# GpSimd norms the last head of rows 8 to 15 ahead of its own scaling, and two blocks of values are copied out of PSUM at other rows of VectorE's loop

## Chip, cores, metric

One core of one Trainium2 chip runs the whole program. The metric is the device time of one execution in microseconds. Five engines work side by side, each through its own list of instructions in order: TensorE (PE in the profile, its weight loads PEld), VectorE (DVE), ScalarE (ACT), GpSimd (POOL) and SyncE (SP, which issues transfers). They wait for each other through semaphores.

## What is computed

The reference is a chain of four residual blocks over x of shape 16 x 128 x 256: a gated attention with four heads, a quantized feed-forward, a second attention with 16 heads, and a mixture of experts. The change is where the first block ends. There, every head of 64 numbers is normed and scaled before it is added to x:

```
mean = jnp.mean(h, axis=-1, keepdims=True)
var = jnp.mean((h - mean) ** 2, axis=-1, keepdims=True)
h_norm = (h - mean) * jax.lax.rsqrt(var + 1e-05)
h_norm = h_norm * outnorm_scale.reshape(1, NH, 1, DH)
...
x = x + _L0_xattn_ref(_layernorm(x, axis=-1), ctx_1024, ctx_1024, ...)
x = x + _L0_ffn_ref(_layernorm(x, axis=-1), ...)
```

The quantized feed-forward needs one largest absolute value over the whole normed x before its first product. Beside all this, keys and values of the second attention, which depend on the context alone, are projected early.

## The kernel before

The 16 rows of x ("row" below is one of the NB = 16 blocks of 128 positions x 256 numbers, held with the positions on the 128 partitions) pass through each stage in order. Between 72 and 116 us of the span the engines do this:

- ScalarE norms the heads of row b in place, `head_norm(b)` (L615): four instructions of 128x64 for rows 0 to 7, three for rows 8 to 15 (HB = 8). Between rows it evicts the keys of a chunk of four rows, `keys(c)` (L621): chunk 0 behind row 3, chunk 1 behind row 7, chunk 2 behind row 13, chunk 3 behind all rows.
- GpSimd multiplies row b by the scale, `h_scale(b)` (L468, one 128x256 instruction), when ScalarE has signalled `h_normed` for the row, and for rows 8 to 15 when VectorE has signalled `last_normed` too.
- VectorE walks a loop over t = 0 to 16: `last_head(t + 2)` (L1129, the fourth head of rows 8 to 15), `add_heads(t)` (L1133, x plus the scaled heads, waits for `h_scaled`), `stats2(t - 1)` (L1137, the statistics of the new x). Where t is 6 and 14 it also runs `values_kept(1)` and `values_kept(2)` (L1119): two instructions each, which take the values of a chunk out of the two banks of pC and add a bias.
- TensorE projects keys and values in four chunks, `keys_values(c)`: 8 matmuls of keys (L1674) and 16 of values (L1683). The values of chunk c go into the banks of pC when VectorE has emptied them of chunk c - 1: `pe.wait_ge(s["v_kept"], 2 * (c - 1) + i + 1)`.

Then comes the turn stage. VectorE forms mean and rstd of all rows, norms each into XL (L956) and takes its largest absolute value (L1163), with `values_kept(3)` in between. TensorE transposes each normed row (L1696) and beside it nine pairs of weight blocks (L1608). ScalarE evicts these (L645, L628), behind `keys(3)`, which waits for the last values (`v_done`). At the end TensorE turns the largest values (L1706) once all rows are evicted and VectorE has the maximum of each partition (L1172), and after a few small steps the products of the feed-forward (L1727) begin.

The order within every engine is written out by hand, as the code below shows.

Of the kernel before, what the change touches and what calls it, by code (L numbers as in the profile page):

```python
# [12 lines left out]
ALU = mybir.AluOpType  # L13
# [52 lines left out]
def at(t, b):  # L66

    if isinstance(b, int):
        return t[:, b]
    ap = t[:, bass.ds(b, 1)]  # L70
    return ap.squeeze(1)


def cols(b, n):

    return bass.ds(b * n, n)
# [9 lines left out]
def build(nc, A, out):  # L86
    x_d = A["x"].rearrange("b s d -> s b d")
    ctx_d = A["ctx_1024"].rearrange("b s d -> s b d")
    NB, S, D = A["x"].shape
    KD = D // P  # L90
    NH0 = A["L0_xattn_igate_bias"].shape[0]
    DH0 = D // NH0
# [16 lines left out]
    with ctx:  # L109
        def sb(name, shape, dt=F32):  # L110
            return ctx.enter_context(nc.sbuf_tensor(name, shape, dt))
# [53 lines left out]
        def view(o, *shape):  # L165
            n = int(np.prod(shape))
            names = "abcd"[:len(shape)]
            ap = arena[:, o:o + n]
            if len(shape) == 1:
                return ap  # L170
            kw = {names[k]: shape[k] for k in range(1, len(shape))}
            return ap.rearrange(f"p ({' '.join(names)}) -> p {' '.join(names)}", **kw)
# [4 lines left out]
        HU = view(0, NB, NH0, DH0 + 1)  # L177
# [50 lines left out]
        mean = sb("mean", [P, NB * NH0])  # L228
        rstd = sb("rstd", [P, NB * NH0])
# [59 lines left out]
        s = Sems()  # L289
# [19 lines left out]
        HB = NB // 2  # L309
# [115 lines left out]
        def _(pool):  # L425
# [35 lines left out]

            pool.wait_ge(s["late_in"], 16 * 6)

            def h_scale(b, u, h):
                pool.wait_ge(s["h_normed"], b + 1)
                if b >= HB:
                    pool.wait_ge(s["last_normed"], b - HB + 1)
                nc.gpsimd.tensor_tensor(at(HN, b), at(HN, b), oscale[:, :].rearrange("p (h d) -> p h d", h=NH0), ALU.mult).then_inc(s["h_scaled"], 1)  # L468
            for b in range(NB):
                h_scale(b, 0, 0)  # L470
# [434 lines left out]
        def _(dve):  # L905
            link = chain(dve, "dve_chain")
            V_ = nc.vector
# [208 lines left out]
            def values_kept(c):  # L1116
                for i in range(2):
                    dve.wait_ge(s["v_done"], 2 * c + i + 1)
                    V_.tensor_tensor(V[:, 4 * c + 2 * i:4 * c + 2 * i + 2, :, 0:DH1], pC[:, i, :].rearrange("p (b h d) -> p b h d", b=2, h=NH1),  # L1119
                                     bv[:, :].rearrange("p (h d) -> p h d", h=NH1).unsqueeze(1).broadcast_to([P, 2, NH1, DH1]), ALU.add).then_inc(s["v_kept"], 1)  # L1120
# [4 lines left out]
            values_kept(0)  # L1125
            head_scale(1)

            def last_head(b, u, h):
                V_.tensor_scalar(at(HU, b)[:, NH0 - 1, 0:DH0], at(HU, b)[:, NH0 - 1, 0:DH0], mean[:, cols(b * NH0 + NH0 - 1, 1)], rstd[:, cols(b * NH0 + NH0 - 1, 1)], ALU.subtract, ALU.mult).then_inc(s["last_normed"], 1)  # L1129

            def add_heads(b, u, h):
                dve.wait_ge(s["h_scaled"], b + 1)
                V_.tensor_tensor(at(X, b).rearrange("p (h d) -> p h d", h=NH0), at(X, b).rearrange("p (h d) -> p h d", h=NH0), at(HN, b), ALU.add).then_inc(s["x1_ready"], 1)  # L1133

            def stats2(b, u, h):
                dve.wait_ge(s["x1_ready"], b + 1)
                V_.bn_stats(at(ST, b), at(X, b)).then_inc(s["row_stats"], 1)  # L1137
            for t in range(NB + 1):
                if HB <= t + 2 < NB:
                    last_head(t + 2, 0, 0)  # L1140
                if t < NB:
                    add_heads(t, 0, 0)
                if t >= 1:
                    stats2(t - 1, 0, 0)
                if t in (6, 14):
                    values_kept(1 + t // 14)
            dve.wait_ge(s["row_stats"], NB)
            moments(4, NB, D)

# [252 lines left out]
            u = (NB - 1) % 2  # L1402
# [749 lines left out]
```

## Time and profile before

| what | value |
|---|---|
| median of 3 runs | 599.08 us (598.14 to 599.44) |
| the profiled execution, its own time | 596.75 us |
| its span, first to last instruction | 595.0 us |
| PE busy | 514.5 us, 86% |
| DVE busy | 379.0 us, 64% |
| ACT busy | 324.4 us, 55% |
| POOL busy | 141.0 us, 24% |
| mean granted clock of TensorE | 0.949 |

The shares are means over the span and say little of one stage. In the rows further down, times are in microseconds from the start of the span. In a row of the timeline, the first number is the start and the second the duration, xN says how many like instructions were merged, and the bracket tells how long the engine sat idle before and who released it. The time of an instruction on VectorE includes what it spends blocked after its issue.

### The profile page before, as it was taken

What the parts mean: (1) busy time and instruction counts of PE and PEld (TensorE: products, weight loads), DVE (VectorE), ACT (ScalarE), POOL (GpSimd) and SP (SyncE); (2) the same over time, 40 slices, a digit from 0 to 9 for tenths busy, and PEclk for the clock granted to TensorE, in tenths of its full rate; (3) what the DMA queues carried; (4) which work ended last, traced back from release to release, by engine and by line L of the source; (5) the groups of instructions that cost most, each with busy time, mean ns of one, the idle gap of its engine ahead of it and who ended that gap; (6) DMA issues with size and microseconds to landing.
All of it is one profiled execution on the core that took longest, in us unless ns stands there. A gap on an engine that the chain in (4) does not pass through costs nothing.

```text
span 595.0 us, 9287 instructions
## 1 busy us (share of the span) xinstructions
PE 514.5 (86%) x3284; PEld 362.9 (61%) x3284; DVE 379.0 (64%) x956; ACT 324.4 (55%) x682; POOL 141.0 (24%) x202
## 2 busy tenths in 40 slices
PE   1989997899999502999989999995799999999994
PEld 1568755644444202887657787874667776777673
DVE  6586998854499989779679699987413332143101
ACT  2866496733499969761398899984212112211220
POOL 2025633000000000000323223111235344534431
PEclk9999998999999955799999999998799999999997
DMA  7900000000000000034000101015134535453410
GB/s 227 298 19 1 2 1 1 1 0 1 0 0 1 0 0 1 0 122 162 2 1 1 38 2 37 1 38 177 28 115 120 183 126 199 120 181 123 132 44 22
DMA packets 31994, 37.58 MB, mean 63 GB/s; under 512 B 8656, under 2 KB 27728, under 8 KB 31952
## 3 DMA queue, kind: packets, MB, share of 16 engines
q1 hardware_dynamic: 28880, 29.07, 15.1%
q0 software_dynamic: 3072, 7.95, 4.6%
q8 instruction: 26, 0.43, 0.3%
q14 instruction: 16, 0.13, 0.1%
HBM read 30.14 MB, written 6.88 MB: 62 GB/s over the span
## 4 chain that ended last, share of the span: by engine, by line
PE 67%; DVE 15%; ACT 10%; issue 3%; POOL 2%; DMA 1%; POOLq 0%; DVEq 0%
PE pA L2103 12%; PE pB L2121 9%; PE pC L1772 6%; PE pC L1811 5%; PE pA L1805 3%; PE pB L1821 3%; PE pA L1727 2%; PE pC L1727 2%; PE pB L1727 2%; ACT XIT L712 2%; PE pC L2114 2%; DVE am L1220 2%; PE pB L1901 2%; DVE arena L1216 2%; DVE am L1186 2%
## 5 line engine op out<-in xcount | busy, mean ns | idle before, releaser
L480 POOL TENSOR_TENSOR arena<-KT,par 128x256 f32<-128x256 f32 x32 | 19.0, 613 | 248.7 <-DVE XIT L1294 186.8
L2103 PE MATMUL pA<-arena 128*128 128x320 f32 x256 | 74.1, 438 | 0.4 <-ACT arena L888 0.4
L900 ACT ACTIVATE arena<-pA 128x320 f32<-128x320 f32 x64 | 28.0, 437 | 71.8 <-PE pA L2103 71.8
L2121 PE MATMUL pB<-arena 128*128 128x256 f32 x256 | 59.3, 385 | 0.0
L2103 PEld LDWEIGHTS pA<-arena 128*128 128x128 f32 x256 | 47.4, 190 | 18.9 <-issue 1.1
L2121 PEld LDWEIGHTS pB<-arena 128*128 128x128 f32 x256 | 47.4, 190 | 9.4 <-issue 3.1
L1186 DVE TENSOR_REDUCE am<-arena 128x1 f32<-128x512 f32 x48 | 32.1, 682 | 23.0 <-ACT arena L652 22.9
L1772 PE MATMUL pC<-wdnT,XIT 128*128 128x256 f32 x192 | 43.6, 385 | 0.8 <-DVE XIT L1294 0.8
L1370 DVE TENSOR_REDUCE rm<-pA 128x16 f32<-128x2048 f32 x16 | 36.7, 2291 | 8.8 <-PE pA L1805 8.8
L1772 PEld LDWEIGHTS pC<-wdnT,XIT 128*128 128x128 f32 x192 | 36.6, 193 | 6.9 <-DVE XIT L1294 1.6
L1811 PE MATMUL pC<-ident,arena 128*128 128x128 f32 x240 | 35.4, 280 | 1.5 <-ACT XIT L748 0.8
L516 POOL DMA_INDIRECT out<-arena,token x24 | 23.5, 977 | 55.2 <-DVE arena L1518 48.0
L785 ACT ACTIVATE arena<-pC 128x512 f32<-128x512 f32 x60 | 34.9, 605 | 0.9 <-PE pC L1811 0.9
L1503 DVE COPY gcol<-arena 128x3 f32<-128x3 f32 x8 | 1.4, 172 | 53.2 <-DMA arena<-token_rows,token 53.2
L514 POOL DMA_INDIRECT arena<-token_rows,token x24 | 24.2, 1010 | 43.7 <-DVE token L1492 25.6
L1811 PEld LDWEIGHTS pC<-ident,arena 128*128 128x128 f32 x240 | 26.1, 141 | 10.5 <-ACT arena L772 4.6
L1538 PE MATMUL pB<-ident 128*128 128x128 f32 x64 | 12.9, 379 | 21.6 <-DVE arena L1267 21.6
L1379 DVE TENSOR_TENSOR arena<-pA,rm 128x1024 f32<-128x1024 f32 (+1 forms) x32 | 29.2, 952 | 0.5
L893 ACT ACTIVATE arena<-pA 128x320 f32<-128x320 f32 x14 | 5.4, 435 | 44.1 <-PE pA L2087 44.1
L772 ACT ACTIVATE arena<-arena 128x1024 f32<-128x1024 f32 (+1 forms) x32 | 28.1, 881 | 0.0
L514 POOL DMA_INDIRECT arena<-out,token x24 | 23.7, 986 | 9.2 <-issue 7.0
L1538 PEld LDWEIGHTS pB<-ident 128*128 128x128 f32 x64 | 11.9, 286 | 21.7 <-issue 21.6
(341 smaller groups left out, 1156.3 us busy)
## 6 DMA issues: line engine op xcount, KB each, us to landing
arena<-in_L_ffn_wi SPq DMA_DIRECT2D x8, 1024.0 KB, 5.3
arena<-in_L_ffn_wo SPq DMA_DIRECT2D x8, 1024.0 KB, 5.6
X<-in_x SPq DMA_DIRECT2D x4, 512.0 KB, 5.6
arena<-in_ctx SPq DMA_DIRECT2D x4, 512.0 KB, 7.2
out<-X SPq DMA_DIRECT2D x4, 512.0 KB, 3.0
token_rows<-arena SPq DMA_DIRECT2D x4, 512.0 KB, 5.2
arena<-in_L_ffn_w_up SPq DMA_DIRECT2D x1, 768.0 KB, 7.7
arena<-in_L_ffn_w_gate SPq DMA_DIRECT2D x1, 768.0 KB, 9.4
```

What stands on the lines that cost most here:

```text
L514: return nc.gpsimd.indirect_dma_start(out=sbuf[0:n, c, :], out_offset=None, in_=dram, in_offset=where, bounds_check=NB * S - 1, oob_is_err ...
L772: nc.scalar.activation(part, part, ACT.Exp).then_inc(s["p_ready"], 1)
L785: nc.scalar.activation(PT[:, u, 4 * g:4 * g + 4, :], bank.rearrange("p (k n) -> p k n", k=4), ACT.Copy).then_inc(s["pt_ready"], 1)
L900: nc.scalar.activation(HT[:, u, f, :], ps[2 + f % 2][:, 0:ROWS], ACT.Relu).then_inc(s["h_relu"], 1)
L1186: V_.tensor_reduce(am[:, 0 if name == "gate" else 1, cols(c * FT + f, 1)], t[:, f, cols(c, 512)], AX.X, ALU.max, apply_absolute_value=True ...
L1370: V_.tensor_reduce(rm[:, u, :], sco, AX.X, ALU.max, negate=True).then_inc(s["rm_ready"], 1)
L1379: V_.tensor_tensor(PR[:, u, part], sco[:, part], rm[:, u, part].unsqueeze(2).broadcast_to([P, part.stop - part.start, P]), ALU.add).then_i ...
L1727: last = mm(ps[2 + f][:, :], w[:, k, f * P:(f + 1) * P], XITv[:, k, cols(c, 512)], start=(k == 0), stop=(k == KD - 1))
L1772: last = mm(ps[6 + u][:, 0:D], OT[:, u, f, :], wdnT[:, f, :], start=(f == 0), stop=(f == FT - 1))
L1811: last = tr(bank[:, n * P:(n + 1) * P], PR[:, u, 4 * g + n, :], ident[:, :])
L2103: last = mm(ps[2 + f % 2][:, 0:ROWS], WI[:, u, k, f * P:(f + 1) * P], XET[:, u, k, :], start=(k == 0), stop=(k == KD - 1))
L2121: last = mm(ps[4 + c][:, 0:D], HT[:, u, f, c * P:(c + 1) * P], WO[:, u, f, :], start=(f == 0), stop=(f == NFT - 1))
```

## The change

The fourth head of rows 8 to 15 is normed by GpSimd, with mean and rstd as operands of each partition, directly ahead of its scaling of the same row. VectorE's instruction for it is gone. `values_kept(1)` moves from the turn t = 6 of VectorE's loop to t = 4, `values_kept(2)` from t = 14 to t = 9.

```diff
             pool.wait_ge(s["late_in"], 16 * 6)
 
+            def last_head(b):
+                if b == HB:
+                    pool.wait_ge(s["head_stat"], 2)
+                nc.gpsimd.tensor_scalar(at(HU, b)[:, NH0 - 1, 0:DH0], at(HU, b)[:, NH0 - 1, 0:DH0], mean[:, cols(b * NH0 + NH0 - 1, 1)], rstd[:, cols(b * NH0 + NH0 - 1, 1)], ALU.subtract, ALU.mult).then_inc(s["last_normed"], 1)
+
             def h_scale(b, u, h):
+                if b >= HB:
+
+                    last_head(b)
+                    pool.wait_ge(s["last_normed"], b - HB + 1)
                 pool.wait_ge(s["h_normed"], b + 1)
-                if b >= HB:
-                    pool.wait_ge(s["last_normed"], b - HB + 1)
                 nc.gpsimd.tensor_tensor(at(HN, b), at(HN, b), oscale[:, :].rearrange("p (h d) -> p h d", h=NH0), ALU.mult).then_inc(s["h_scaled"], 1)
...
-            def last_head(b, u, h):
-                V_.tensor_scalar(at(HU, b)[:, NH0 - 1, 0:DH0], at(HU, b)[:, NH0 - 1, 0:DH0], mean[:, cols(b * NH0 + NH0 - 1, 1)], rstd[:, cols(b * NH0 + NH0 - 1, 1)], ALU.subtract, ALU.mult).then_inc(s["last_normed"], 1)
-
...
             for t in range(NB + 1):
-                if HB <= t + 2 < NB:
-                    last_head(t + 2, 0, 0)
                 if t < NB:
                     add_heads(t, 0, 0)
                 if t >= 1:
                     stats2(t - 1, 0, 0)
-                if t in (6, 14):
-                    values_kept(1 + t // 14)
+                if t == 4:
+                    values_kept(1)
+                if t == 9:
+                    values_kept(2)
```

On GpSimd, at the end of its first scalings, the list was this before (arena is the buffer of the heads):

```order
L468 TENSOR_TENSOR arena<-arena,oscale 128x4x64 [waits h_normed,late_in]
L468 TENSOR_TENSOR arena<-arena,oscale 128x4x64 [waits h_normed] x7
L468 TENSOR_TENSOR arena<-arena,oscale 128x4x64 [waits last_normed,h_normed] x8
```

It is this now:

```order
L475 TENSOR_TENSOR arena<-arena,oscale 128x4x64 [waits h_normed] x7
L467 TENSOR_SCALAR arena<-arena,mean,rstd 128x64 [waits head_stat]
L475 TENSOR_TENSOR arena<-arena,oscale 128x4x64 [waits h_normed,last_normed]
L467 TENSOR_SCALAR arena<-arena,mean,rstd 128x64
L475 TENSOR_TENSOR arena<-arena,oscale 128x4x64 [waits h_normed,last_normed]
```

The pair of the last two rows repeats up to row 15; each scaling now waits for the small instruction just ahead of it on the same engine.

On VectorE, around the last rows of the loop (turns 13 to 16, then the first sum of the moments), the list was this before:

```order
L1133 TENSOR_TENSOR X<-X,arena 128x256 [waits h_scaled]
L1137 BN_STATS ST<-X 128x6 [waits x1_ready]
L1133 TENSOR_TENSOR X<-X,arena 128x256 [waits h_scaled]
L1137 BN_STATS ST<-X 128x6 [waits x1_ready]
L1119 TENSOR_TENSOR V<-pC,bv 128x32x16 [waits v_done] x2
L1133 TENSOR_TENSOR X<-X,arena 128x256 [waits h_scaled]
L1137 BN_STATS ST<-X 128x6 [waits x1_ready] x2
L914 TENSOR_TENSOR s<-ST 128x16 [waits row_stats]
```

It is this now, from turn 9 on (one pair of add and statistics for each of turns 10 to 14 where the dots are):

```order
L1137 TENSOR_TENSOR X<-X,arena 128x256 [waits h_scaled]
L1141 BN_STATS ST<-X 128x6 [waits x1_ready]
L1126 TENSOR_TENSOR V<-pC,bv 128x32x16 [waits v_done] x2
L1137 TENSOR_TENSOR X<-X,arena 128x256 [waits h_scaled]
...
L1141 BN_STATS ST<-X 128x6 [waits x1_ready] x2
L921 TENSOR_TENSOR s<-ST 128x16 [waits row_stats]
```

The two copies of values that stood between the adds of rows 14 and 15 now stand behind the add of row 9.

## Rows read from the trace of the kernel before

**Rows 1.** The chain that ended last, 97 to 117 us: start, duration, what

```profile
97.36 0.69 POOL arena L468
98.08 0.43 DVE X L1133
98.50 0.34 DVE ST L1137
98.84 0.60 DVE V L1119
99.48 5.42 PE pC L1683 x16
104.93 1.27 ACT KT L621 x2
...
114.84 0.56 ACT XIT L645 x2
115.40 0.24 issue
```

**Rows 2.** Timeline of DVE: add 10, copies, add 15, then the turn stage

```profile
92.96 0.43 DVE L1133 TENSOR_TENSOR X<-X,arena 128x256 f32<-128x256 f32 x1
98.75 1.27 DVE L1119 TENSOR_TENSOR V<-pC,bv 128x512 f32<-128x512 f32 x2
99.94 0.42 DVE L1133 TENSOR_TENSOR X<-X,arena 128x256 f32<-128x256 f32 x1
103.38 0.73 DVE L956 TENSOR_SCALAR arena<-X,mean,rstd 128x256 f32<-128x256 f32 x2
115.09 0.17 DVE L1172 TENSOR_REDUCE gm<-am 128x1 f32<-128x16 f32 x1
```

**Rows 3.** Timeline of POOL: scalings of rows 8, 10, 14 and 15

```profile
90.25 0.68 POOL L468 TENSOR_TENSOR arena<-arena,oscale 128x256 f32<-128x256 f32 x1 [1.46 <-ACT arena L615]
92.24 0.69 POOL L468 TENSOR_TENSOR arena<-arena,oscale 128x256 f32<-128x256 f32 x1 [0.31 <-ACT arena L615]
97.36 0.68 POOL L468 TENSOR_TENSOR arena<-arena,oscale 128x256 f32<-128x256 f32 x1 [1.44 <-ACT arena L615]
98.36 0.69 POOL L468 TENSOR_TENSOR arena<-arena,oscale 128x256 f32<-128x256 f32 x1 [0.31 <-ACT arena L615]
```

**Rows 4.** Timeline of PE: values of chunks 2 and 3, keys between, first turn

```profile
88.90 3.72 PE L1683 MATMUL pC<-F,KT 128*128 128x256 f32 x16 [1.37 <-DVE V L1119]
92.46 3.60 PE L1674 MATMUL pB<-KT,F 128*128 128x512 f32 x8
99.48 5.41 PE L1683 MATMUL pC<-F,KT 128*128 128x256 f32 x16 [3.43 <-DVE V L1119]
```

**Rows 5.** Costliest groups, POOL alone, by form: count, busy, mean ns

```profile
L503 POOL TENSOR_SCALAR XIT<-XIT 128x256 f32<-128x256 f32 x1 | 0.9, 864 | 0.1
L440 POOL TENSOR_SCALAR_AFFINE_SELECT ident<-ident 128x128 f32<-128x128 f32 x1 | 0.3, 289 | 0.2 <-POOL ident L439 0.2
L437 POOL MEMSET arena<- 128x64 f32 x1 | 0.2, 204 | 0.0
L500 POOL IOTA XIT<- 128x16 f32 x1 | 0.1, 143 | 0.0
```

**Rows 6.** Timeline of DVE and of POOL at 84 to 86 us

```profile
84.19 0.89 DVE L1133 TENSOR_TENSOR X<-X,arena 128x256 f32<-128x256 f32 x1
85.34 0.40 DVE L1133 TENSOR_TENSOR X<-X,arena 128x256 f32<-128x256 f32 x1
84.12 0.68 POOL L468 TENSOR_TENSOR arena<-arena,oscale 128x256 f32<-128x256 f32 x1 [1.79 <-ACT arena L615]
85.45 0.84 POOL L468 TENSOR_TENSOR arena<-arena,oscale 128x256 f32<-128x256 f32 x1 [0.65 <-ACT arena L615]
```

**Rows 7.** Windows, busy and count of PE, PEld, DVE, ACT, POOL, then granted clock

```profile
99.00:100.00 1.00, 0.52 (x2) 0.49 (x3) 1.00 (x3) 0.00 (x0) 0.04 (x1) 1.00 0.00 0
101.00:102.00 1.00, 1.00 (x4) 0.78 (x3) 0.90 (x8) 0.00 (x0) 0.00 (x0) 0.50 0.00 0
103.00:104.00 1.00, 1.00 (x3) 0.74 (x3) 0.93 (x4) 0.00 (x0) 0.00 (x0) 0.50 0.00 0
105.00:106.00 1.00, 0.76 (x8) 0.53 (x5) 1.00 (x5) 1.00 (x2) 0.00 (x0) 1.00 0.00 0
```

## Prediction

> **What bounds the kernel now.** I read the chain of waits first, to see through which engine the end of this stage is reached, then the timelines of VectorE, GpSimd and TensorE around it, because the chain shows only one of several paths of nearly equal length.
>
> The chain runs from GpSimd's scaling of row 14 through VectorE's add of that row, into the copies of values, over TensorE's last 16 value matmuls, to the last keys on ScalarE, and then along ScalarE's evictions to the end of the turn stage [rows 1]. TensorE had been idle 3.43 us for the copies, and the matmuls took 5.41 us where those of chunk 2 took 3.72 [rows 4]: the granted clock fell to 0.5, the 1.2 GHz level, after that idle stretch and was back at 1.0 when the turn stage began [rows 7].
>
> That makes the copies look worth 3 or 5 us. They are not, since a second path ends beside it. VectorE starts to norm rows at 103.38 and has its last maximum at 115.09 + 0.17 = 115.26 [rows 2], and it does so whatever TensorE does. ScalarE's last eviction ends at 115.40 and the turn of the maxima starts 0.24 later, at 115.64 [rows 1]. So if ScalarE had been earlier, the end would still be at 115.26 + 0.24 = 115.50. The first 0.14 us belong to TensorE and ScalarE; everything beyond must come from VectorE's start at 103.38.
>
> What sets that start is row 15. Its scaling ends at 98.36 + 0.69 = 99.05 [rows 3], but its add starts at 99.94, because the two copies of values stand in front of it, from 98.75 on [rows 2]. An add that is free to go starts 0.03 us behind its scaling: row 10's scaling ends at 92.24 + 0.69 = 92.93 and its add starts at 92.96, row 14's ends at 98.05 and its add starts at 98.08 [rows 1 to 3]; all adds from row 8 to row 14 follow GpSimd by that distance.
>
> **The change part by part.**
>
> VectorE's eight norms of the last head: removed, worth nothing by themselves. In rows 8 to 14 VectorE already stands waiting for GpSimd at every add, as just shown; a shorter list only waits longer. If that cover were gone, they would be eight times a few tenths.
>
> The copies of chunk 2, from turn 14 to turn 9: row 15's add may start at 99.05 + 0.03 = 99.08 instead of 99.94, which is 0.86 us. At turn 9 they put 98.75 to 99.94, 1.19 us, in front of the add of row 10. From one add to the next there are 1.0 us, the pace of GpSimd's starts (90.25, and 92.24 two rows on [rows 3]), and the work in it, add and statistics, starts 0.34 apart [rows 1, 2], so 0.67 us. VectorE wins back 0.3 us each row and is on time again by row 14, ahead of which ScalarE puts the keys of chunk 2 and GpSimd idles 1.44 us [rows 3].
>
> The copies of chunk 1, from turn 6 to turn 4: the values of chunk 2 start when their keys are done, 1.37 us sooner than 88.90 [rows 4], so at 87.5. TensorE goes on without a stop: values until 91.1, keys until 94.7, and with the copies of chunk 2 done by about 94.0 the last values from 94.7 to 98.3. The last keys on ScalarE then run before the turn stage. Worth: the 0.14 us of above.
>
> GpSimd's norms: this is the unknown. No row shows a 128x64 tensor_scalar with operands of each partition there. Below, it can't be shorter than a memset of that size, 0.20; above, not longer than the 128x256 tensor_scalar, 0.86; a 128x16 iota of 0.14 is nearly all fixed cost, and 0.12 fixed plus a quarter of the other 0.74 gives 0.31; a 128x128 select with one input is at 0.29 [rows 5]. It has two operations and must fetch its operands, so I take d = 0.35.
>
> How the norm is packed beside VectorE matters too. An add and a scaling block each other: the add issued at 84.19, just behind the scaling of 84.12, took 0.89 instead of some 0.42, so its reading began about 0.14 before the scaling's end at 84.80; and the scaling issued at 85.45 into the add of 85.34 took 0.84 instead of 0.68 [rows 6]. With the change, GpSimd starts the norm of row b + 1 just as its scaling of row b ends (some 0.04 before its end, as instructions there follow each other), and the add of row b comes 0.03 after that end. The add is held until the norm is nearly through, d - 0.04 - 0.14, then reads for 0.30, and the next scaling starts behind that: d + 0.12 after the end of the last one. The semaphore from norm to scaling fits into that (an idle of 0.24 between two dependent instructions [rows 5] would make it d + 0.20, its upper price). So GpSimd needs 0.69 + 0.35 + 0.12 = 1.16 us each row, where ScalarE delivers one each 1.0 us.
>
> The Trainium skill, page "SBUF — State Buffer", section "Who interferes with whom", says that a VectorE instruction with two SBUF inputs and a GpSimd instruction that reads SBUF share an exclusive lock, and that the second fully blocks until the first is done; the trace agrees in both directions, but for the 0.14. Held to the full ends, add behind norm and scaling behind add, a row would cost 0.35 - 0.04 + 0.34 + 0.69 = 1.34. [...]
>
> The sum. Row 8's norm falls into the idle before 90.25, so its scaling ends at 90.93 as before. Five rows later, row 13's ends at 90.93 + 5 x 1.16 = 96.73; row 14's would at 97.89, but has to wait for ScalarE and ends at 98.04 as before. Row 15's ends at 98.04 + 1.16 = 99.20, its add starts at 99.23 instead of 99.94: VectorE is 0.71 us early into the moments and through the turn stage. With the 0.14 the stage ends 0.85 us sooner. All behind it is the same program. The profiled execution would take 596.75 - 0.85 = 595.9; it stands 2.33 under the median shown, and on that median I forecast 599.08 - 0.85 = **598.2 us**.
>
> The point at which GpSimd eats the gain: if its pace binds all seven rows, row 15 ends at 90.93 + 7P. The add would be no sooner than before at P = (99.94 - 0.03 - 90.93)/7 = 1.28, and the stage even at P = 1.30, so d = 0.49. Beyond it each 0.1 in d costs 0.7 us. At the top bound d = 0.86, P = 1.67, row 15 ends at 102.6, the add 2.7 late, the time 2.6 above. At the bottom, d = 0.20, P = 1.01: gain 1.0.
>
> **The rivals.**
>
> A. GpSimd becomes the bound of the adds. For it: seven-fold leverage, an idle of only 0.31 us before each scaling now [rows 3], the 864 ns of the one tensor_scalar there. Against: a quarter of its size. At d = 0.6, P = 1.41, row 15 ends at 100.8, its add 0.86 late: 599.8. With the lock held to full ends (P = 1.34): row 15 ends 100.31, add 0.40 late, 599.3. This is the case on the other side; it decides from d = 0.49.
>
> B. TensorE's clock in the turn stage. TensorE now ends its values at 98.3 and idles until the first normed row, at about 103.1: longer than the 3.43 us behind which the clock fell. It was then at 0.5 until after 104, with work since 99.48 [rows 4, 7]. As much work before it rises puts the low stretch until about 108, where transposes and weight turns go at half the rate. ScalarE's evictions need 115.4 - 106.2 = 9.2 us [rows 1] and could now start at 103.2, so they have about 2 us of slack before VectorE's end at 114.6; I estimate that the low stretch uses most of it and costs 0 to 0.7. Should the clock stay low to the end of the stage, the cost is 3 us or more: 601 to 602. VectorE feeds TensorE steadily and in the stage it was busy throughout, which speaks against it.
>
> C. The change gives nothing: VectorE is late at row 15 for another reason, or A and B eat just what is won: 599.0.
>
> D. More than forecast: if low clock stretches elsewhere in the program fall more kindly, 597.5. The rows of this stage allow 1.0 at most.
>
> **How the numbers follow.** The forecast, 0.5 to 1.0 sooner, 0.45. A, 0.22, over half of it beyond 1.2 us late only if d exceeds 0.65. B's long form 0.06. C 0.15. D 0.12. A measurement here tells about 0.2%, 1.2 us, from no change. Faster by more: D, and part of the forecast by scatter of the runs, which spread 1.3 us: 0.20. Slower by more: upper half of A and B: 0.20. Within: 0.60. The range goes from 597.1 (forecast with D) to 600.4 (A at d = 0.65, and the mild end of B). The likeliest case's own is 597.7 to 598.7.
>
> **What would show it.** Right: GpSimd's norm at 0.3 to 0.4 us; scalings of rows 9 to 13 about 1.15 apart; row 15's add at about 99.2 on the old scale; TensorE without a stop from 84 to 98 and idle until 103; VectorE's maximum as the last wait of the turn stage. Wrong: a norm above 0.5 us, adds of rows 9 to 15 sliding ever later behind GpSimd, or the turn stage's transposes at a clock of 0.5 past 108 with ScalarE the last to finish.

## The result

The changed kernel takes 601.18 us in the median of 22 runs (598.71 to 602.76), the kernel before 599.22 us (596.58 to 600.26): ratio 1.0031, 95% interval 1.0019 to 1.0043. It is slower by about 0.3%, 1.9 us, where the prediction had it 0.85 us faster. Of all the runs reported below, two of the six of e1 were far slower than the rest (608.96 and 2940.57 us), and no median or ratio here counts them.

The profiled execution of the changed kernel took 602.04 us, its span 600.3 us. That of before (596.75 us) stood 2.5 us under its own median, so the two spans, 5.3 us apart, overstate the change; what is comparable is a stretch between two fixed points of the program. I use the stretch from GpSimd's first scaling (row 0) to the turn of the largest values that ends the turn stage.

GpSimd's timeline of the changed kernel, from the norm of row 8 to the scaling of row 11, then the scaling of row 15; the bracket is the idle time before:

```profile
89.97 0.86 POOL L467 TENSOR_SCALAR arena<-arena,mean,rstd 128x64 f32<-128x64 f32 x1
91.35 0.68 POOL L475 TENSOR_TENSOR arena<-arena,oscale 128x256 f32<-128x256 f32 x1 [0.53 <-ACT arena L622]
92.02 0.85 POOL L467 TENSOR_SCALAR arena<-arena,mean,rstd 128x64 f32<-128x64 f32 x1
92.95 0.69 POOL L475 TENSOR_TENSOR arena<-arena,oscale 128x256 f32<-128x256 f32 x1
93.62 0.85 POOL L467 TENSOR_SCALAR arena<-arena,mean,rstd 128x64 f32<-128x64 f32 x1
94.55 0.68 POOL L475 TENSOR_TENSOR arena<-arena,oscale 128x256 f32<-128x256 f32 x1
95.22 0.58 POOL L467 TENSOR_SCALAR arena<-arena,mean,rstd 128x64 f32<-128x64 f32 x1
95.88 0.68 POOL L475 TENSOR_TENSOR arena<-arena,oscale 128x256 f32<-128x256 f32 x1
...
102.27 0.68 POOL L475 TENSOR_TENSOR arena<-arena,oscale 128x256 f32<-128x256 f32 x1
```

Each L467 is one norm, each L475 a scaling. The norm takes 0.84 to 0.86 us, not 0.35, and in one row 0.58. Scalings that followed each other by 1.0 us [rows 3] now do so by 1.6 (by 1.33 in the row with the short norm), with less than 0.1 us of idle time on GpSimd between two instructions: ScalarE, which set the pace, is no longer waited for. VectorE's timeline over the same stretch, adds and copies alone:

```profile
92.07 0.43 DVE L1137 TENSOR_TENSOR X<-X,arena 128x256 f32<-128x256 f32 x1 [1.29 <-POOL arena L475]
93.67 0.43 DVE L1137 TENSOR_TENSOR X<-X,arena 128x256 f32<-128x256 f32 x1 [0.84 <-POOL arena L475]
94.35 1.27 DVE L1126 TENSOR_TENSOR V<-pC,bv 128x512 f32<-128x512 f32 x2
95.53 0.42 DVE L1137 TENSOR_TENSOR X<-X,arena 128x256 f32<-128x256 f32 x1
...
102.99 0.43 DVE L1137 TENSOR_TENSOR X<-X,arena 128x256 f32<-128x256 f32 x1 [0.84 <-POOL arena L475]
```

But for row 10's, in front of which the copies now stand, every add starts 0.03 or 0.04 us after its scaling ends, and VectorE idles 0.83 or 0.84 us ahead of it in five of the seven rows from 9 on. GpSimd's first scaling stood at 77.05 before and at 78.09 now, so all of this trace is 1.04 us late from before the change's place. Row 15's add at 102.99 is at 101.95 on the scale of before, where it was at 99.94 [rows 2]: 2.01 us late.

TensorE's timeline shows the other half of the change doing what was forecast:

```profile
88.40 3.62 PE L1687 MATMUL pC<-F,KT 128*128 128x256 f32 x16
91.85 3.60 PE L1678 MATMUL pB<-KT,F 128*128 128x512 f32 x8
95.29 3.62 PE L1687 MATMUL pC<-F,KT 128*128 128x256 f32 x16
106.90 0.69 PE L1700 MATMUL pA<-ident,arena 128*128 128x128 f32 x2 [8.00 <-DVE arena L963]
...
119.13 0.27 PE L1710 MATMUL pA<-ident,gm 128*1 128x128 f32 x1 [0.74 <-ACT XIT L652]
```

The two waits of [rows 4] are gone, the last 16 value matmuls take 3.62 us instead of 5.41. But TensorE then has nothing to do for 8.0 us. The windows (busy time and count of PE, PEld, DVE, ACT, POOL, then the granted clock) show what that brings:

```profile
100.00:102.00 2.00, 0.00 (x0) 0.00 (x0) 1.17 (x4) 0.00 (x0) 1.92 (x3) 1.00 0.00 0
104.00:106.00 2.00, 0.00 (x0) 0.00 (x0) 1.31 (x10) 0.87 (x3) 0.00 (x0) 0.50 0.00 0
110.00:112.00 2.00, 2.00 (x11) 2.00 (x10) 2.00 (x7) 1.35 (x4) 0.00 (x0) 0.50 0.04 8
114.00:116.00 2.00, 1.99 (x16) 1.60 (x17) 2.00 (x7) 2.00 (x7) 0.00 (x0) 1.00 0.00 0
```

TensorE's last value matmuls end at 98.91. In windows of half a microsecond the clock is last at 1.0 at 101.5 to 102.0 and first at 1.0 again at 112.5 to 113.0, work having begun again at 106.90: it fell to the 1.2 GHz level some 3.3 us after the last work and stayed there for the first 5.5 us of the turn stage. In that time TensorE is the bound (2.00 of 2.00 busy) and ScalarE waits for it (1.35 of 2.00).

The stretch from row 0's scaling to the turn of the maxima took 115.64 - 77.05 = 38.59 us before and 119.13 - 78.09 = 41.04 after: 2.45 us more. Of that, VectorE's lateness is 2.01. How the turn follows VectorE is best read where neither the last values nor the clock are late, as in e10 below:

```profile
113.90 0.75 ACT L645 ACTIVATE XIT<-pA 128x256 f32<-128x256 f32 x2
114.43 0.17 DVE L1174 TENSOR_REDUCE gm<-am 128x1 f32<-128x16 f32 x1
114.91 0.27 PE L1710 MATMUL pA<-ident,gm 128*1 128x128 f32 x1 [0.68 <-ACT XIT L645]
```

The maximum ends at 114.60 and the last eviction at 114.65; the turn starts 0.31 us behind the one and 0.26 behind the other, and so it does in e6 and e12. In the chain of these traces the last evictions hang on VectorE's late norms, by way of TensorE's transposes. So VectorE's list sets the end of the stage, but the wait that ends last is for ScalarE, in all fourteen traces. In the changed kernel the maximum starts at 118.14 and takes 0.17, so the turn could start at 118.62; it waits for ScalarE until 119.13, 0.51 more, which is the low clock: e5, the same kernel with the clock held at 1.0, has these 0.51 back. Before, the same sum gave 115.26 + 0.31 = 115.57 against 115.64, 0.07 for the late values, which are gone: 2.01 + 0.51 - 0.07 = 2.45. From the turn to VectorE's maximum at 211.33, now at 214.82, both traces take 95.69 us. The last 1.8 us of the difference of the spans come later, where this execution has a stretch of low clock that the one of before has not (0.57 at 450 to 454 us).

### The profile page after: what moved, and what is told of

Read it like the earlier page. It is cut to its first block, busy times and chain, and to the rows that moved or that the text cites. A ratio compares the mean times of both kernels' runs of the same rounds, so it can differ in the third digit from the quotient of the medians.

```text
span 600.3 us, 9287 instructions
## 1 busy us (share of the span) xinstructions
PE 515.6 (86%) x3284; PEld 365.3 (61%) x3284; DVE 376.6 (63%) x948; ACT 324.9 (54%) x682; POOL 147.9 (25%) x210
## 4 chain that ended last, share of the span: by engine, by line
PE 67%; DVE 15%; ACT 9%; issue 2%; POOL 2%; DMA 2%; POOLq 0%; SPq 0%; DVEq 0%
PE pA L2107 12%; PE pB L2125 9%; PE pC L1776 6%; PE pC L1815 5%; PE pA L1809 3%; PE pB L1825 3%; PE pA L1731 2%; PE pC L1731 2%; PE pB L1731 2%; ACT XIT L719 2%; PE pC L2118 2%; DVE am L1224 2%; PE pB L1905 2%; DVE arena L1220 2%; DVE am L1190 2%
## 5 line engine op out<-in xcount | busy, mean ns | idle before, releaser
L2125 PE MATMUL pB<-arena 128*128 128x256 f32 x256 | 60.9, 393 | 0.0
```

The costliest lines, as they stand in the source:

```text
L2125: last = mm(ps[4 + c][:, 0:D], HT[:, u, f, c * P:(c + 1) * P], WO[:, u, f, :], start=(f == 0), stop=(f == NFT - 1))
```

## The experiments

Each kernel was timed in turns with the kernel before on the same chip. The column "stretch" is the one just defined, read from the kernel's own trace, less the 38.59 us of before.

| kernel | median us, kernel before | ratio, 95% interval | stretch |
|---|---|---|---|
| the change | 601.18, 599.22 | 1.0031, 1.0019 to 1.0043 | +2.45 |
| e1, copies alone | 596.82, 599.05 | 0.9958, 0.9943 to 0.9972 | -0.59 |
| e2, norm alone | 602.50, 599.05 | 1.0053, 1.0040 to 1.0066 | +3.83 |
| e3, norms spread | 597.68, 599.05 | 0.9972, 0.9959 to 0.9986 | -0.66 |
| e4, copies and 36 matmuls | 597.25, 599.05 | 0.9974, 0.9962 to 0.9986 | +0.22 |
| e5, the change and 32 matmuls | 600.18, 598.67 | 1.0041, 1.0020 to 1.0062 | +1.94 |
| e6, copies of chunk 2 alone | 597.67, 598.67 | 0.9984, 0.9966 to 1.0001 | -0.93 |
| e9, before and 13 matmuls | 600.22, 598.67 | 1.0027, 1.0008 to 1.0046 | -0.06 |
| e10, copies and 18 matmuls | 598.04, 598.67 | 1.0000, 0.9983 to 1.0017 | -0.93 |
| e11, e1 once more | 597.29, 598.55 | 0.9988, 0.9967 to 1.0009 | -0.63 |
| e12, last copies later too | 597.72, 598.55 | 0.9984, 0.9965 to 1.0002 | -2.11 |

e7 and e8 have one execution each, at 598.81 and 599.45 us; their stretches, -0.02 and -0.03, repeat that of before, as both leave the stage as it was.

The ratios do not follow small differences of the stretch: e4, whose stage is longer than before, has 0.9974, e10, whose stage is 0.93 us shorter, has 1.0000, and e12, 2.11 us shorter, has 0.9984. What is said of parts of a microsecond below rests on the traces, one for each kernel.

### e1: the copies alone

```diff
-                if t in (6, 14):
-                    values_kept(1 + t // 14)
+                if t == 4:
+                    values_kept(1)
+                if t == 9:
+                    values_kept(2)
```

> The kernel before with the copies of values at turns 4 and 9 alone; VectorE keeps the last head's norm. Theory (GpSimd's norm, 0.85 us instead of the 0.35 I took, is the whole loss): row 15's add starts 0.03 us behind its scaling, some 0.85 us sooner than before, and the kernel is 0.7 to 1.0 us faster than before (ratio about 0.9985). Rival 1 (the early copies make TensorE idle from 98 to 103 us and the turn stage run at the low clock): the turn stage's last wait is on ScalarE and the time is 0 to 1 us slower than before. Rival 2 (the copies at turn 9 hold up adds and VectorE never recovers): row 15's add is not sooner.

Faster, ratio 0.9958; this ratio rests on four runs of the kernel, fewer than the others, and e11 repeats it. In VectorE's timeline the last two adds are:

```profile
98.43 0.43 DVE L1133 TENSOR_TENSOR X<-X,arena 128x256 f32<-128x256 f32 x1 [0.53 <-POOL arena L468]
99.43 0.43 DVE L1133 TENSOR_TENSOR X<-X,arena 128x256 f32<-128x256 f32 x1 [0.24 <-POOL arena L468]
```

This trace starts its first scaling at 77.42, 0.37 later than before, so row 15's add is at 99.06 on the scale of before, 0.88 us sooner; I had worked out 0.86. VectorE is on time again by row 14, as its idle of 0.53 shows. So rival 2 is out. Rival 1 is out as the main cause, but it has a part: the turn of the maxima waits for ScalarE here too, and the stretch is 0.59 shorter, not 0.88 + 0.07. The turn starts at 115.42, where VectorE's maximum (114.58 + 0.17) would have let it start at 115.06, so 0.36 are lost again: -0.88 - 0.07 + 0.36 = -0.59. The windows of TensorE (busy and count, then clock) show why:

```profile
102.00:104.00 2.00, 0.67 (x3) 0.50 0.01 4
106.00:108.00 2.00, 2.00 (x11) 0.50 0.00 0
```

### e2: the norm alone

The change, with the `values_kept` lines as in the kernel before.

> The change with the copies left at turns 6 and 14, so only the norm moves to GpSimd. Theory: scalings of rows 9 to 15 follow each other by 1.6 us, row 15's scaling ends near 101.9 on the scale of before, the add of row 15 comes behind the copies at about 102.2, TensorE's last values start at about 101.6 after 5.6 us of idling, and the time is 2.0 to 2.8 us above before (ratio about 1.004), a few tenths above the changed kernel. Rival 1 (clock through early copies is the cause): near before, within 1 us.

The slowest of all, ratio 1.0053, and the stretch 3.83 us longer. The eight norms take 0.60 to 0.85 us (0.60 is the first, beside which VectorE is at its copies) and the scalings are again 1.6 apart. Here the copies still stand before row 15's add, TensorE waits longer for them, and the last keys reach ScalarE only behind them. It was expected 2.0 to 2.8 above before and came out at 3.2 with an interval of 2.4 to 4.0. The norm alone is the loss; the copies take part of it back.

### e3: the same eight norms where GpSimd idles

```diff
                 if b >= HB:
-                    last_head(b)
                     pool.wait_ge(s["last_normed"], b - HB + 1)
...
+            BEHIND = {4: (8,), 5: (9,), 6: (10,), 7: (11, 12), 8: (13,), 13: (14, 15)}
             for b in range(NB):
                 h_scale(b, 0, 0)
+                for r in BEHIND.get(b, ()):
+                    last_head(r)
```

> The change with GpSimd's eight norms put where it idles: behind the scalings of rows 4 to 8 (rows 8 to 13) and 13 (rows 14 and 15). Theory: a norm alone takes 0.58 us, and the scalings of rows 9 to 13 are 1.0 us apart again, row 15's add starts some 0.8 us sooner than before, and the time is as in the run with the copies alone, 0.7 to 1.0 us under before. Rival 3 (any norm on GpSimd costs, because it blocks VectorE's adds wherever it stands): 0.5 us or more above that run.

Ratio 0.9972, stretch -0.66, as with the copies alone. GpSimd's timeline, scalings of rows 12 and 13, norms of rows 14 and 15, scaling of row 14:

```profile
96.66 0.68 POOL L473 TENSOR_TENSOR arena<-arena,oscale 128x256 f32<-128x256 f32 x1 [0.31 <-ACT arena L623]
97.65 0.69 POOL L473 TENSOR_TENSOR arena<-arena,oscale 128x256 f32<-128x256 f32 x1 [0.31 <-ACT arena L623]
98.32 1.41 POOL L467 TENSOR_SCALAR arena<-arena,mean,rstd 128x64 f32<-128x64 f32 x2
99.80 0.69 POOL L473 TENSOR_TENSOR arena<-arena,oscale 128x256 f32<-128x256 f32 x1
```

The scalings wait for ScalarE again (0.31), 1.0 apart, and two norms fit into the gap before row 14. So it is not the norm's engine that costs, but its place: eight norms on GpSimd cost nothing where it idles, and 3.1 us of the stretch (2.45 against -0.66) in a list that has 0.31 us to spare per row. They also win nothing over e1, which keeps them on VectorE: its time for them was covered, as the prediction said. Rival 3 is out.

### e4, e10 and e5: TensorE kept at work before the turn stage

```diff
             for c in range(4):
                 keys_values(c)
+            keep_busy(ps[2], 18)
```

36 in e4 and 18 in e10, on top of e1; 32 in e5, on top of the change. They multiply the unit matrix into an unused bank and add nothing to the result.

> The copies at turns 4 and 9 alone, and 36 matmuls of 128x128 on an unused bank between the last values and the first turn, some 3.9 us at full clock, to keep TensorE from idling. They add nothing to the result. Theory: the granted clock stays 1.0 through the turn stage; the end of the stage is set by VectorE either way, so the time is that of the run with the copies alone or 0 to 0.3 us less. Rival 1: 1 us or more below the run with the copies alone.

In e4 I had mistaken the size: each of the 36 is two passes in the trace, and they held TensorE until 109.1, so it came about 3 us late to the first turn.

```profile
101.02 8.20 PE L1540 MATMUL pA<-ident 128*128 128x128 f32 x72
109.06 0.38 PE L1700 MATMUL pA<-ident,arena 128*128 128x128 f32 x2
```

With the clock at 1.0 all through the turn stage, the stretch is still only 0.22 longer than before and 1.15 longer than in e10: the stage absorbs more than half of a late start, if the clock is high.

> The copies at turns 4 and 9 alone, with 18 extra matmuls behind the last values, some 4.1 us of work (the 36 of the run before this were 72 passes and took 8.2 us, so TensorE came 3 us late to the turn stage). They add nothing to the result. Theory: clock 1.0 through the turn stage, VectorE ends it, 0.3 to 0.5 us below the run with the copies alone; if the clock matters more in other executions than in the profiled ones, 1 us or more below.

> The changed kernel with 32 extra matmuls of 128x128 on an unused bank behind the last values, some 7.2 us of work in the 8.0 us in which TensorE idles there. They add nothing to the result. Theory: the clock stays at 1.0 in the turn stage and VectorE instead of ScalarE ends it; that part of the change's loss was 0.6 us, so the time is 0.4 to 0.8 us below the changed kernel and still 1 us or more above before (ratio 1.001 to 1.003). Rival 1 (the clock is the larger part): at or below before.

In both, the clock stayed at 1.0 in the turn stage. The stretch is 0.34 us shorter than in e1 and 0.51 shorter than in the change, as the 0.36 and 0.51 that the low clock cost there by the sums above. That part of both expectations held. The times did not follow: e10's ratio is 1.0000 where e1's was 0.9958 and 0.9988, and e5's is 1.0041 where the change has 1.0031, with intervals that overlap, but for those of e10 and the first e1. Keeping TensorE at work won nothing here that the timings show.

### e6: the copies of chunk 2 alone

Only `values_kept(2)` is moved, from t = 14 to t = 9.

> The kernel before with the copies of chunk 2 alone moved, to turn 9; those of chunk 1 stay at turn 6. Theory: what counts is that nothing stands in front of row 15's add and that the last values are done before the turn stage; TensorE's last values run from 96 to 100 and both hold, so the time is within 0.3 us of the run with both copies moved. If the copies of chunk 1 matter by themselves, it is 0.5 us or more above that.

Ratio 0.9984 and the stretch is the shortest of the kernels without extra work, -0.93. TensorE ends its values later than in e1 and idles 3.49 us, not 5.11. The clock falls here too, but only during the stage, for 3.4 us (106.3 to 109.7), where e1 has the first 5.2 us of the stage at the low clock (103.3 to 108.5), and the stage absorbs that: VectorE's list sets its end. Moving the copies of chunk 1 has no worth of its own, and in the trace costs a third of a microsecond through the clock.

### e9 and e8: is there more in the kernel before than its profile shows?

> The kernel before with 13 extra matmuls of 128x128 on an unused bank between the keys and the values of the last chunk, 2.9 us of work in the 3.43 us in which TensorE waits for the copies. They add nothing to the result. It asks why the copies alone won some 2 us in time where the stage in the two profiles is only 0.6 us apart. Theory L (in most executions of the kernel before the low stretch behind that idle time lasts longer than in the profiled one, and the last values and the first turns run in it): 1 us or more faster than before. Rival (VectorE's start is all that counts, and the rest is scatter): within 0.4 us of before.

> The kernel before once more, to see how a second execution of it differs from the profiled one. If the differences between the profiles outside the stage are scatter, the stretch from GpSimd's first scaling to the turn of the maxima takes 38.6 us again (115.64 - 77.05), within 0.1, and the start and the rest differ by up to some 3 us with stretches of low clock at other places. If theory L holds, the stretch itself is 0.5 us or more longer.

e1's first ratio was three times what its stage shows, so I asked whether the profiled execution of before was a lucky one inside the stage. It was not. In e8 the first scaling starts at 80.17 and the turn at 118.73, a stretch of 38.56 us. e7, the kernel before with extra work only behind the turn, has 38.57. What differs is the start: the first scaling of e8 is 3.1 us later. TensorE's windows of e8 and of the first trace of before at 34 to 38 us:

```profile
34.00:38.00 4.00, 3.27 (x15) 0.71 0.00 0
```

```profile
34.00:38.00 4.00, 3.70 (x36) 1.00 0.00 0
```

A stretch of low clock in the first stage goes with it. It came in eight of the other traces too; those of the change, e1, e7 and e10 have none, like the first of before. In the five traces without it the first scaling starts at 77.05 to 78.53, in the nine with it at 79.42 to 80.59. Stretches like this, outside the place of the change, may be much of the 4 us by which the runs of one kernel spread; that is not shown, as most executions have no trace. e9 removes the wait behind which the clock fell, its stretch is 0.06 shorter, its time is not better but worse (1.0027). Theory L is out, but the rival's "within 0.4 us" did not come either. Why e9 is slower is open.

### e7: what the norm costs by itself

24 instructions behind the last scaling, while GpSimd has nothing else to do and the other engines go on with the first products; they write numbers that nobody reads.

```diff
+            pool.wait_ge(s["gate_out"], 4)
+            m, r, c = oscale[:, 64:65], oscale[:, 65:66], oscale
+            for n in range(4):
+                nc.gpsimd.tensor_scalar(forms[:, n * 64:n * 64 + 64], c[:, 0:64], m, r, ALU.subtract, ALU.mult)
+            for n in range(4, 8):
+                nc.gpsimd.tensor_scalar(forms[:, n * 64:n * 64 + 64], c[:, 0:64], 0.5, 2.0, ALU.subtract, ALU.mult)
...
```

> The kernel before with 24 extra instructions on GpSimd while nothing else uses it, during the first products of the feed-forward; they write numbers that nobody reads. Four each of: the norm's form (128x64, two operations, operands of each partition), the same with constants, one operation with a constant, a product of two tensors of 128x64, the norm's form at 128x16 and at 128x256. It asks what the 0.58 us of the lone norm are. If they are the price of fetching the operands, the form with constants takes 0.3 us or less; if fixed cost of the instruction, all tensor_scalars of 128x64 take 0.5 to 0.6, the 128x16 about 0.5 and the 128x256 about 0.9; if cost of each element, the 128x16 takes about 0.25 and the 128x256 2 us.

The groups by line, with the shortest, median and longest in ns: the norm's form, the same with constants, one operation with a constant, a product of two tensors, then the norm's form at 16 and at 256 columns.

```profile
L476 POOL TENSOR_SCALAR arena<-oscale x4: 568/570/593, 129.4 to 131.1; 128x64 f32<-128x64 f32 x4
L478 POOL TENSOR_SCALAR arena<-oscale x4: 418/418/419, 131.6 to 132.8; 128x64 f32<-128x64 f32 x4
L480 POOL TENSOR_SCALAR arena<-oscale x4: 357/358/366, 133.2 to 134.1; 128x64 f32<-128x64 f32 x4
L482 POOL TENSOR_TENSOR arena<-oscale x4: 308/308/312, 134.5 to 135.3; 128x64 f32<-128x64 f32 x4
L484 POOL TENSOR_SCALAR arena<-oscale x4: 423/598/1368, 135.6 to 137.6; 128x16 f32<-128x16 f32 x4
L486 POOL TENSOR_SCALAR arena<-oscale x4: 1215/1216/1217, 138.0 to 141.6; 128x256 f32<-128x256 f32 x4
```

The norm alone takes 0.57 us. From 64 to 256 columns it grows by 646 ns, 3.4 ns per column, so 0.22 us of the 64 columns are the columns and 0.35 are fixed; the shortest at 16 columns, 0.423, lies within 0.02 of that. The first two of the 16-column row, 1.37 from 135.61 and 0.77 from 136.45, run beside two instructions of VectorE, and the first of these is longer too (its like take 0.74 in the trace of before); the two behind them take 0.42:

```profile
135.15 1.02 DVE L1196 TENSOR_SCALAR XIT<-XIT,sc 128x1024 f32<-128x1024 f32 x1
136.20 0.73 DVE L1198 TENSOR_SCALAR XIT<-XIT 128x1024 f32<-128x1024 f32 x1
```

Operands of each partition cost 0.15 over constants, the second operation 0.06. Of the three guesses, fixed cost is the largest part at 64 columns, but the form matters: one operation with a constant, at 256 columns, is 0.86 ([rows 5]: L503 is that form), the norm's form 1.22.

### e11 and e12

> The copies at turns 4 and 9 alone, the same kernel as in the first set of runs, measured once more, because its gain there (ratio 0.9958) is three times what its stage shows and the runs of the second set (same stage, ratios 0.9984 and 1.0) say less. If the stage is all, the ratio comes out at 0.999 to 0.998; if early copies win more than the stage shows, at 0.996 again.

Ratio 0.9988 (0.9967 to 1.0009), stretch -0.63, against 0.9958 and -0.59 the first time. The stage repeats to 0.04 us, the ratio doesn't. The gain of the copies alone is best read as the stage's 0.6 us, with the ratios of e1, e6 and e11 all at or below that; by the timings alone it can't be told from 2 us. So of the two outcomes in the expectation the first came.

e12 goes one step further along the same list: `values_kept(3)` leaves VectorE's turn stage.

```diff
-                if t == 4:
-                    values_kept(3)
...
             x_int(0)
+            values_kept(3)
             for c in range(4):
                 gate_chunk(c)
...
-            pe.wait_ge(s["v_kept"], 8)
             pe.wait_ge(s["xit_ready"], NB)
...
+                    elif f == 4:
+                        pe.wait_ge(s["v_kept"], 8)
```

> The copies at turns 4 and 9, the 18 extra matmuls behind the last values, and the copies of chunk 3 taken out of VectorE's turn stage and put behind the first integers of the feed-forward, where VectorE waits 2.7 us. Theory (VectorE's list from row 15's add to the last maximum sets the stage's end): VectorE is 1.19 us earlier, ScalarE with 9.2 us of evictions from 103.2 becomes the last at about 112.8, and the stage ends 1.0 to 1.3 us sooner than with the copies alone and the matmuls, some 2.1 us sooner than before. Rival: the copies behind the integers delay the first maxima of the products, or ScalarE is the bound already, and nothing is won.

The stretch went from 37.66 in e10 to 36.48 us, 1.18 less, for copies of 1.19: VectorE's list does set the stage's end. ScalarE did not become the bound, as I had thought; the turn starts 0.31 behind the end of VectorE's maximum (116.59 + 0.17, the turn at 117.07), as in e10, and the chain runs through VectorE's norms. But right behind it the clock fell. The windows of TensorE:

```profile
115.00:117.00 2.00, 1.25 (x9) 1.00 0.00 0
119.00:121.00 2.00, 2.00 (x11) 0.50 0.00 0
```

The 16 filling matmuls took 3.27 us instead of 2.05 and the next maxima were 1.4 us later relative to the turn (214.16 - 117.07 = 97.09 against 95.69). That is not a price of the moved copies: e4 (216.29 - 119.19 = 97.10) and e7 (214.19 - 117.10 = 97.09) lose the same 1.4 us at the same place, with the copies of chunk 3 where they always were, and all eleven other traces have 95.68 or 95.69. e7's window of TensorE:

```profile
119.00:121.00 2.00, 2.00 (x11) 0.50 0.00 0
```

e7's program is that of before up to this point, so the low stretch comes in some executions of a kernel and not in others. Whether e12 draws it more often than the rest is open. The ratio is 0.9984 (0.9965 to 1.0002), no more than e6's.

## Why the prediction was wrong

**The failed step is the term d, "so I take d = 0.35".** Alone the norm is 0.57 us, and beside VectorE's adds 0.85. The prediction's own formula for a late GpSimd has the right shape and overstates the loss: its "top bound d = 0.86" had P = 1.67, the add 2.7 late and 2.6 us above; measured were P = 1.60 in all rows but one, 2.01 late, and, with 0.51 from the clock, a stretch 2.45 longer. Rival A was the case that came, beyond the d = 0.65 up to which I let the range reach.

The term was mis-sized in two parts. First, "0.12 fixed plus a quarter of the other 0.74": the slope was about right (2.9 ns per column against 3.4), the fixed part was taken from an iota and is 0.35 for this form. The 128x256 tensor_scalar of [rows 5], the 0.86 that was both split and taken as the top bound, is one operation with a constant. For that form the quarter was nearly right (0.31 against the 0.36 of e7 at 64 columns); the norm's form costs 0.57 at 64 columns and 1.22 at 256, so 0.86 was no bound. With 0.57 alone, the formula has P = 1.38 and the add of row 15 at 100.62, 0.68 late; the rest is the second part, the packing with the add. "The add of row b ... is held until the norm is nearly through" was the wrong way round. The add, issued 0.05 us behind the norm, is not held (0.43 us as ever), and it is the norm that grows, from 0.58 to 0.85, when an add starts with it. The one norm at 0.58 in the first fence above is the one that started while VectorE was at the copies (94.35 to 95.53), with the add coming 0.3 us later; the norms of 0.60 in e2 (at 92.19), 0.58 in e3 (at 88.64) and 0.58 in e5 (at 97.15) also stand beside copies. That the norm reads its two operand columns first and finds the add reading when it comes to its tensor would explain it; no run shows that. The rule that the prediction cited from the Trainium skill ("SBUF — State Buffer", "Who interferes with whom") has the instruction that starts first block the other; in these rows the norm starts first and is the one that pays, so the rule as I used it did not tell who pays. Its sum, 1.34 a row with d = 0.35, would with d = 0.57 be 1.56, close to the 1.60 measured, but by luck: in that sum the add waits for the norm, and here it doesn't.

**"VectorE's eight norms of the last head: removed, worth nothing"** was right: e1 and e3 have the same stretch within 0.07.

**The copies, "0.86 us" and "VectorE wins back 0.3 us each row"**: right, 0.88 in e1. The 0.14 beside it was 0.07, since the turn follows VectorE's maximum by 0.31 and not by the 0.24 I took from ScalarE's row. The sign "VectorE's maximum as the last wait" came in no trace, as ScalarE's last eviction ends 0.05 behind it even where VectorE's list sets the pace. The next point took more than the 0.07 back.

**Rival B, "costs 0 to 0.7"**: it came in addition to A, at 0.51 in the change and 0.36 in e1. I had priced it and then left it out of the sum, though its condition (a longer idle than the one that had lowered the clock in the trace) was met by the forecast itself. Its "low stretch until about 108" came true: in e1 the clock rose at about 108.5, 108.1 on the scale of before.

**The leverage.** The prediction named "beyond it each 0.1 in d costs 0.7 us" and still gave the whole case 22%. With bounds of 0.20 and 0.86 on d and a turning point at 0.49, half of the interval lay on the losing side, and its upper end was too low. (At d = 0.6 the sum gives an add 0.89 late, where the prediction has 0.86.)

## What to carry to other kernels

An instruction put into the list of an engine that others wait for is paid in every turn of the loop once it is longer than that engine's idle time (0.31 us here), so compare the two before counting what it frees elsewhere; placed in real gaps, the same instructions cost nothing. Before a row serves as a bound, read from the code that it has the form in question. When a cost is known only between two bounds and is multiplied by seven, start the chance of the losing case from the share of the interval beyond the turning point. And where one execution is 2 us off its median, compare stretches between fixed points of the program, not spans.

## What the runs showed of the hardware

- A GpSimd tensor_scalar with two operands of each partition takes 0.57 us at 64 columns and 1.22 at 256, so 0.35 us plus 3.4 ns per column (e7); with one operation and a constant it takes 0.36 and 0.86. A product of two tensors at 64 columns is cheaper (0.31) than a subtraction of a constant (0.36).
- An add of VectorE with both inputs in SBUF, issued 0.05 us behind such an instruction, takes its usual 0.43 us, and the instruction takes 0.85 instead of 0.58; issued behind a GpSimd product, it is itself held (0.89 us in [rows 6], and again 0.89 at 85.23 in the changed kernel).
- GpSimd's 128x16 form took 1.37 us instead of 0.42 beside VectorE's 128x1024 tensor_scalars, of which one took 1.02 instead of 0.74 (e7).
- A low stretch of TensorE's clock costs what the stage can't absorb: 3.4 us of it in the turn stage cost nothing in e6, 5.2 us cost 0.36 in e1, 5.5 us cost 0.51 in the change. Low stretches come at other places from one execution of a program to the next: behind the turn in e4, e7 and e12, each time for 1.4 us, and in the first stage in nine of fourteen traces. What decides where the clock falls stays open, and so does why e9 is slower than the kernel before.
